# A perceiver block on one core: transposes and copies at the head in another order, low parts and key banks around the third normalisation moved

## What is computed

```python
x = x + xattn(ctx, _layernorm(x), Wq, bq, Wk, bk, Wv, bv, gamma, beta)
x = x + attn(_layernorm(x), q_weight, v_weight, out_w, out_b)
x = x + ffn(_layernorm(x), w_q, w_k, w_gate, value_experts, output_experts)
```

## Time and profile before

| | before |
|---|---|
| median of 3 runs | 600.45 us (600.14 to 600.69) |
| the profiled execution | 603.26 us |
| its span, first to last instruction | 601.5 us |
| PE busy | 580.8 us (97% of the span) |
| DVE, ACT, POOL busy | 352.8, 201.6, 215.3 us |
| PE's named waits | 6.2 us before its first matmul, 10.7 us in the others |
| chain that ended last | PE 90%, DVE 5%, issue 2%, ACT 1%, DMA 1%, POOL 1% |

### The profile page before, as it was taken

How to read it: one execution, slowest core, us unless ns; L and a number is a source line. 1 busy time by engine, 2 the same in 40 slices (tenths; PEclk the granted TensorE clock), 3 DMA queues, 4 the chain that set the end, 5 groups by cost and what they waited for, 6 DMA issues and landing times.

```text
span 601.5 us, 11465 instructions
## 1 busy us (share of the span) xinstructions
PE 580.8 (97%) x4860; PEld 499.2 (83%) x4864; DVE 352.8 (59%) x410; ACT 201.6 (34%) x286; POOL 215.3 (36%) x182
## 2 busy tenths in 40 slices
PE   5989999999999999999999999899999999999997
PEld 5979889898989889796778988787778888888886
DVE  5679481735547181742696256757677546875641
ACT  3453342505334341514502442323343112433320
POOL 2566764564626265560324000202333444000000
PEclk9989999999999999999989889999999999999999
DMA  8770524141223324005002401023922232698601
GB/s 313 265 279 2 212 80 148 70 143 42 102 79 91 127 70 148 2 7 192 10 2 72 149 3 60 13 70 95 247 86 71 89 121 71 144 242 226 159 1 70
DMA packets 25140, 65.76 MB, mean 109 GB/s; under 512 B 2408, under 2 KB 2408, under 8 KB 22160
## 3 DMA queue, kind: packets, MB, share of 16 engines
q1 hardware_dynamic: 25104, 65.23, 34.6%
HBM read 64.05 MB, written 1.18 MB: 108 GB/s over the span
## 4 chain that ended last, share of the span: by engine, by line
PE 90%; DVE 5%; issue 2%; ACT 1%; DMA 1%; POOL 1%; DVEq 0%
PE ps L317 17%; PE ps L318 17%; PE ps L319 17%; PE ps L827 4%; PE ps L830 4%; PE ps L814 3%; PE ps L818 3%; PE ps L820 2%; PE ps L816 2%; PE ps L815 2%; PE ps L819 2%; PE ps L822 2%; PE ps L829 2%; PE ps L882 2%; PE ps L844 1%
## 5 line engine op out<-in xcount | busy, mean ns | idle before, releaser
L454 POOL TENSOR_TENSOR psum_tmp<-psum_tmp,raw 128x512 f32<-128x512 f32 (+1 forms) x88 | 132.1, 1501 | 34.3 <-DVE lo L1314 25.8
L317 PE MATMUL ps<-hi,gh 128*128 128x512 f32 x192 | 75.7, 394 | 0.0
L319 PE MATMUL ps<-hi,gl 128*128 128x512 f32 x192 | 74.8, 390 | 0.0
L318 PE MATMUL ps<-lo,gh 128*128 128x512 f32 x192 | 74.8, 390 | 0.0
L1314 DVE TENSOR_TENSOR lo<-raw,hi 128x2048 fp32r<-128x2048 f32 (+1 forms) x29 | 60.1, 2106 | 20.9 <-ACT hi L527 20.9
L508 POOL TENSOR_TENSOR sx<-sx,raw 128x512 f32<-128x512 f32 x32 | 41.0, 1290 | 84.9 <-DVE raw L1642 84.9
L708 ACT ACTIVATE hi<-raw 128x2048 fp32r<-128x2048 f32 x14 | 26.8, 1913 | 91.9 <-PE ps L319 91.9
L317 PE MATMUL ps<-wvh,gh 128*128 128x512 f32 x128 | 51.2, 400 | 0.0
L319 PE MATMUL ps<-wvh,gl 128*128 128x512 f32 x128 | 50.2, 393 | 0.0
L318 PE MATMUL ps<-wvl,gh 128*128 128x512 f32 x128 | 50.2, 392 | 0.0
L1648 DVE TENSOR_TENSOR lo<-raw,hi 128x2048 fp32r<-128x2048 f32 x15 | 34.3, 2289 | 19.9 <-ACT hi L708 19.9
(11 more groups left out here) (224 smaller groups left out, 1380.9 us busy)
## 6 DMA issues: line engine op xcount, KB each, us to landing
raw<-in_ctx SPq DMA_DIRECT2D x23, 1024.0 KB, 4.8
raw<-in_ve SPq DMA_DIRECT2D x8, 1024.0 KB, 5.3
raw<-in_oe SPq DMA_DIRECT2D x8, 1024.0 KB, 5.7
wk<-gm_rows SPq DMA_DIRECT2D x8, 512.0 KB, 9.2
g<-gm_rows SPq DMA_DIRECT2D x8, 512.0 KB, 9.7
raw<-in_ctx SPq DMA_DIRECT2D x8, 130.0 KB
raw<-in_ctx SPq DMA_DIRECT2D x2, 512.0 KB, 4.6
xres<-in_x SPq DMA_DIRECT2D x1, 1024.0 KB, 10.0
```

The lines of the kernel that those rows point to most:

```text
L317: pe.matmul(dst, wh, xh, start=first, stop=False)
L318: pe.matmul(dst, wh, xl, start=False, stop=False)
L319: return pe.matmul(dst, wl, xh, start=False, stop=last)
L454: pool.tensor_tensor(psum_tmp[0:k, :], (raw[:, 0, :] if t == 1 else psum_tmp[0:k, :]), raw[0:k, t, :], ALU.add).then_inc(ctx_sum, 1)
```

## The change

At the head:

- the first chunk is loaded with three DMAs, one tile, one tile, two tiles; tile 0's four products that need high parts alone come first and wait for the high part only;
- `first_transposes(1)` moves from behind the Gram matrix to ahead of its last tile;
- ACT makes the high parts of blocks 2 and 3 before it waits for the end of the Gram matrix, and then copies the triangle before the crossed rows; DVE makes the low parts of blocks 2 and 3 before `cross_copy`;
- `value_query_products` moves ahead of `g_transposes(0)`.

Around the third normalisation:

- `w_low` of the query weights moves ahead of `near_norm(3)` on DVE, the gate weights' high and low parts ahead of `near_high(2)` and `near_low(2)`;
- `norm_front(3, 2)` moves ahead of `xT_pair_low(2, 0)`; POOL's `memset` waits until all four tiles are normalised;
- keys lie in banks 2, 3, 4, 5; keys 2 and 3 wait for the copies of queries 2 and 3 instead of the gates, and the logits begin when three key copies are done: only the last quarter waits for the fourth.

```diff
-            for t in (0, 2):
-                sp.dma_start(raw[:, t:t + 2, :], ...
+            for t, n, landed in ((0, 1, ld_first), (1, 1, ld_second), (2, 2, ld_ctx[0])):
+                sp.dma_start(raw[:, t:t + n, :], ...
...
+            pool.wait_ge(s_norm[3], NT)
             pool.memset(vals[:, :, :, :], 0.0).then_inc(v_zero, 1)
...
             xT_high(0, (0, 1))
+            xT_high(0, (2, 3))
             act.wait_ge(gram_mm, 4)
+            upper_copy()
             for m in range(2):
                 act.activation(cross[:, m, :], bank[3 + m][:, :], ACT.Copy).then_inc(cr_act, 1)
-            xT_high(0, (2, 3))
-            upper_copy()
...
                         if first and c < CH:
-                            if t < r.stop - 1:
+                            if t == 0:
+                                pe.wait_ge(first_hi, 1)
+                            elif t < r.stop - 1:
...
-                        if first and t == NSLOT - 3:
-                            first_transposes(0)
+                        if first and t >= NSLOT - 3 and t != NSLOT - 2:
+                            first_transposes((t - NSLOT + 3) // 2)
...
+                        if first and start:
+                            for m in range(KC):
+                                high_product(m)
+                            pe.wait_ge(first_lo, 1)
...
             gram(0, True)
-            first_transposes(1)
             first_queries((0,))
             mirror(0)
             first_queries((1,))
+            value_query_products()
             g_transposes(0)
-            value_query_products()
             first_queries((2, 3))
...
-                    mm = three(pe, bank[(2, 3, 0, 1)[c]][:, :], ...
+                    mm = three(pe, bank[2 + c][:, :], ...
...
-                if c == 3:
-                    pe.wait_ge(ge_done, 1)
+                if c >= 2:
+                    pe.wait_ge(q_done, 2 * KC + c + 1)
                 keys(c)
...
-                    pe.wait_ge(k_done, KC)
+                    pe.wait_ge(ge_done, 1)
+                    pe.wait_ge(k_done, KC - 1)
...
                 for n in range(4):
+                    if i == 0 and n == KC - 1:
+                        pe.wait_ge(k_done, KC)
...
             xT_low(0, (0, 1))
+            xT_low(0, (2, 3))
             cross_copy(0, True)
-            xT_low(0, (2, 3))
...
             near_norm(2)
+            w_low(W_Q2, 0)
             near_norm(3)
+            dve.wait_ge(wg_hi_done, 2)
+            dve.tensor_tensor(wg_lo, wg_raw, wg_hi.bitcast(F32), ALU.subtract).then_inc(wg_lo_done, 1)
             near_low(2)
             near_low(3)
...
-            w_low(W_Q2, 0)
-            dve.wait_ge(wg_hi_done, 2)
-            dve.tensor_tensor(wg_lo, wg_raw, wg_hi.bitcast(F32), ALU.subtract).then_inc(wg_lo_done, 1)
...
+            norm_front(3, 2)
             xT_pair_low(2, 0, range(KC))
-            norm_front(3, 2)
```

More of the change, by code:

```diff
@@ L674, in _ @@
             w_high(W_Q2, 0, 2)
+            act.wait_ge(ld_wg, 16)
+            act.wait_ge(wg_hi_done, 1)
+            act.activation(wg_hi, wg_raw, ACT.Copy).then_inc(wg_hi_done, 1)
             near_high(2)
@@ L821, in gram @@
                         w = hi[0:kk, t, block[2]]
-                        pe.matmul(acc[:, 2, 0:2 * P], w, hb[:, 2:4, :], start=start, stop=stop, skip_group_check=True)
+                        if not (first and start):
+                            high_product(2)
                         if start and second:
@@ L828, in gram @@
                         w = hi[0:kk, t, block[3]]
-                        pe.matmul(acc[:, 2, 2 * P:4 * P], w, hb[:, 0:4:3, :], start=False, stop=stop, skip_group_check=True)
+                        if not (first and start):
+                            high_product(3)
                         mm = pe.matmul(mir[:, 1, :], w, lb, start=start, stop=stop, skip_group_check=True)
```

27 lines of the change are left out of this document (16 added, 11 removed).

## The result

| | before | changed |
|---|---|---|
| median of 7 runs each | 600.45 us (598.19 to 602.88) | 593.67 us (591.21 to 595.94) |
| ratio, 95% interval | | 0.9891 (0.9863 to 0.9920) |
| the profiled execution, its span | 603.26, 601.5 us | 591.21, 589.4 us |
| mean granted clock of that span | 0.989 | 0.997 |

The changed kernel is 6.8 us faster by the medians (4.8 to 8.2 by the interval). Runs more than 1.5% above the fastest of their kernel enter no ratio here; there are three, all of the kernel before.

A forecast was written before the change was run, and what follows sets the result against it. PE was busy 580.8 of 601.5 us, so only its waits and low clock could be gained. Head 4.2, third normalisation 2.3 and keys 1.1 sum to 7.6 us: 600.45 to 592.8 us, range 591.0 to 595.6.

The forecast's parts named there:

- Start: Kernel's head: smaller first load and tile 0 not waiting for its low part let PE start 1.0 us earlier.
- Stall ahead of the first queries: Head: with the second transposes inside the Gram matrix, the first queries follow without a wait, 1.9 us gained.
- Low clock behind the stall: Head, first queries: without the wait PE's clock should not drop behind it, 1.7 us gained.
- case 2: Rival: the clock gain of 1.7 us fails, as the drop moves or unprofiled runs never had it; 594.5 us, chance 0.25.
- New wait at batch 0's transposes: Head, ahead of the transposes of the sums: PE waits 0.3 us for DVE's additions, a loss.
- I cost the thinner cover at nothing: Batch 1: DVE's and ACT's parts, paced by POOL's sums, start no earlier, yet PE was to lose 0 us.
- case 3: Rival: ACT's order or DVE's sums hold PE 1.5 us more, normalisation gains only 0.7; 596.0 us, chance 0.12.
- Third normalisation: Third normalisation: queries begin 0.7 us earlier and the 1.56 us wait goes whole, 2.3 us gained.
- three parts of the 1.56 us wait: Third normalisation: tile 2's statistics behind low parts, the late start, and the last scaling slowed beside POOL's memset.
- Keys: Ahead of the logits: mask products and three quarters of the logits cover the fourth key copy, 1.1 us gained.
- The rule on transposes: New head: transposes do not count as PE being busy, so the low clock may only move; sum 5.9 us.
- Case 5: Rival: PE stays at low clock from the new small work on; from 19 us decides against the change; chance 0.02.

The follow-up runs named there:

- e3_sums_first: Changed kernel with DVE's additions for batch 1's Gram sums put ahead of its copy of that batch's context row sum; 594.67 us, ratio 0.9915 to before.

## Why the prediction was right, and where it was not

The sum of 7.6 us and the measured 6.8 (4.8 to 8.2) lie close, and 593.67 lies within 0.9 us of the forecast. But the sum is not right term by term, and that it comes so near is partly luck. At equal clock the change is worth 6.0 ± 0.3 us by the runs. By the segments it is 1.7 at the head (the averages) and 3.5 behind. The clock adds some 0.8.

- **Start, 1.0.** It measured 1.4 in the changed kernel's profile, 1.0 to 1.5 over all, 1.3 on the average. The landing came 0.2 to 0.8 us earlier, 0.6 on the average. I had taken 0.3, "since most of it will be fixed": too little.
- **Stall ahead of the first queries, 1.9.** Right: no wait at 28.38, 1.61 back with the step undone, about 2 us in all. Start and stall together were to bring the first queries 2.9 us forward; by the averages of the profiles it is 2.8.
- **Low clock behind the stall, 1.7.** This step failed in its size and in its reason. I read one profile of before, found a wait and a low stretch behind it, and took the second as the first's price. Three other profiles with the same wait had no such stretch. The runs with the new head have on the average half a stretch less, so the term is about 0.8 and not 1.7. That the timed runs might not have it was named as case 2; the 2.8 us between the profiled execution and the median was the sign for it, and I gave it 0.25.
- **New wait at batch 0's transposes, -0.3.** It did not come in the changed kernel's profile (36.31, no bracket); in that of `e3_sums_first` it was 0.58. DVE's additions began at 30.95, and the sum had them at 31.9.
- **"I cost the thinner cover at nothing".** This step failed, too, by 0.8 to 1.4 us, 1.1 on the average of six profiles. I argued that PE had no wait for DVE's and ACT's parts of batch 1. True, but PE's, ACT's and DVE's work moved forward, POOL's did not, and the two engines hold each other. The mechanism is near case 3's, one batch later than it was looked for. The profile could have warned: the earlier trace rows has additions of DVE at 1.06 and more beside POOL's, and I priced DVE's side of that meeting, not POOL's.
- **Third normalisation, 2.3.** The queries began 0.73 earlier (28.05 to 27.32), the second group another 1.78: 2.5. The three parts of the 1.56 us wait are confirmed by what each undoing brings back: 1.47 for the low parts, without the clock, 0.76 for the `memset`, 0.15 for the statistics, not additive.
- **Keys, 1.1.** It measured 1.0.
- **The rule on transposes.** The stretch over 128 small products, six transposes and the queries behind them has a clock of 1.00. The low stretch did not move there, as the rule of the Trainium skill (TensorE: Matmul & The Clock Gate, Part 4: PE-mode transpose) would have had it. None of the ten profiles without the wait has one there. But as only one of four had it in the old place, this speaks against the rule no more than weakly.
- **Case 5, the low clock that would decide against the change.** The sum adds the 1.7 where it has to be taken off. The limit is 2 x (7.6 - 1.7), about 12 us of low clock, and not 19. No run came near it.

So the sum would have been 7.6 - 0.9 for the clock - 1.1 for the new wait + 0.3 for the one that did not come + 0.1 for the rest: 6.0. The runs have 6.8 by the medians, and 6.0 at equal clock with 0.8 for the clock. The 0.8 us that the segments do not hold are not assigned to a step. The profiled execution was at 591.21 instead of 595.7, for three low stretches fewer (5.2 us), of which my sum had one, and for 0.9 us in a wait at 290 us that comes and goes between profiles: the step that holds it took 21.37 us before and 20.49 after, and in the other twelve profiles either 20.5 to 20.6 or 21.2 to 21.4.

## What to carry to other kernels

Price a clock drop only as a chance unless it comes in several profiles of the same code. The mean granted clock of each run, laid beside its time, shows how many microseconds of a difference are clock; take the mean over many runs, as a median moves in whole stretches. When work is moved forward on one engine, list the work of its neighbour that did not move and now lies beside it: the cost came up one batch later, on an engine that the edit did not touch. When a wait is put down to one meeting of two engines, look whether it stays away in every profile in which they miss each other. A wait that an order only moves can be a sign that two engines together are full there.

## What the runs showed of the hardware that I had not expected

- By the mean granted clock, one and the same program ran with none to six stretches at the lower level, each some 3.4 us long and 1.7 us dear: 595.9 us at a mean clock of 1.000, 603.2 at 0.989. The Trainium skill (TensorE: Matmul & The Clock Gate, Part 1: The HAM clock gate) says of a kernel's start that the number of matmuls at the lower level differs from run to run of one kernel. Here the start differs, too (the pace changes at 8.86 us in one profile and at 11.65 in another), and so does the number of low stretches later on, which made 5.2 of the 12.1 us between two single profiles.
- A low stretch without a named wait in the 10 us ahead of it: in every one of the 14 profiles one lies between 334 and 350 us behind the small products with heads of part 2, and takes 3.4 or 6.8 us (from the first group of part 2's distance products to the last it is 12.33 or 13.95 us). It does not come in every execution: 4 of the 61 timed runs have a mean clock of 1.000.
- DVE and POOL hold each other, and in the pairs seen here the one that began second was held. POOL's addition of 512 columns takes 1.29 us alone, 3.3 to 3.4 when it begins just behind one subtraction of DVE, which then takes its 2.28, and 8.21 behind three that follow each other closely and also take 2.28 each. Where POOL began first, its addition took 1.29 and DVE's subtraction 3.42. DVE's scaling took 2.00 instead of 0.54 beside a `memset`.
